# A fused attention and MLP block on one core: the head-pair loop written out, es transposed behind qe, and each score and weight block taken out of PSUM by one masked product of 384 columns

## The reference, cut to what matters

```python
xn = layernorm(x)
q, k, v, g = (xn @ W.T per head for W in (Wq, Wk, Wv, Wg)); q, k = rope(q), rope(k)
s   = clip(xn @ Ws1.T @ Ws2.T + bs2, -32, 32)        # per head: T x 64
es  = exp(s); enz = 1 / cumsum(es)                   # exp(-cumlogsumexp(s))
A   = tril(q @ k.T * DK ** -0.5)                     # 256 x 256, lower triangle
ok  = enz * (A @ es)
qv  = softmax(ok)
W2  = tril((qv * enz) @ es.T)                        # 256 x 256, lower triangle
o   = W2 @ v
out_a = (rmsnorm(o) * g_norm * silu(g)) @ Wo.T
out_m = (gelu(xn @ Wgate.T) * (xn @ Wup.T)) @ Wdown.T   # 4-bit weights, decoded in the kernel
out = x + out_a + out_m
```

## Time and profile before

| | before |
|---|---|
| Median of 3 runs | 1187.22 us |
| The profiled execution, its own time | 1186.13 us |
| Its span, first to last instruction | 1184.4 us |
| Mean granted TensorE clock, share of full | 0.986 |
| TensorE busy (matmul) | 1114.7 us, 94% |
| VectorE busy | 943.1 us, 80% |
| ScalarE busy | 642.1 us, 54% |
| GpSimd busy | 419.6 us, 35% |

### The profile page before, as it was taken

The page is one execution under the profiler, slowest core; times in us unless marked ns, Lnnn a source line. Parts: engine busy times, 40 slices in busy tenths (PEclk is TensorE's granted clock), DMA queues, the critical chain, the costliest instruction groups (busy, mean ns, idle before and its releaser), DMA issues.

```text
span 1184.4 us, 20879 instructions
## 1 busy us (share of the span) xinstructions
PE 1114.7 (94%) x6872; PEld 941.6 (79%) x6872; DVE 943.1 (80%) x1808; ACT 642.1 (54%) x1748; POOL 419.6 (35%) x306
## 2 busy tenths in 40 slices
PE   6789999999999998999989999899998999999995
PEld 5568888888788887888878888788887888788884
DVE  6888887888868887888877888778886888877763
ACT  5355564655645565555655556464563565655451
POOL 5233242433513335232443324343251433523231
PEclk9899999999999999999999999999999999999998
DMA  4001000100001000010000100001000100000001
GB/s 157 1 1 74 1 1 1 52 22 1 1 2 73 1 1 2 1 73 1 1 3 1 74 1 1 3 16 59 1 1 2 73 1 1 1 2 19 1 19 36
DMA packets 9117, 23.19 MB, mean 20 GB/s; under 512 B 816, under 2 KB 5808, under 8 KB 7984
## 3 DMA queue, kind: packets, MB, share of 16 engines
q1 hardware_dynamic: 9008, 21.76, 5.0%
HBM read 19.66 MB, written 2.10 MB: 18 GB/s over the span
## 4 chain that ended last, share of the span: by engine, by line
PE 71%; issue 8%; DVE 6%; ACT 6%; POOL 3%; POOLq 0%; DVEq 0%; ACTq 0%
PE bank L203 17%; PE bank L205 16%; PE bank L204 16%; PE bank L292 5%; ACT xs L568 3%; PE bank L305 3%; PE bank L349 2%; DVE xs L860 2%; POOL qkT L1087 2%; PE bank L294 2%; DVE Wt L740 2%; ACT xs L567 2%; PE bank L282 1%; PE bank L338 1%; PE bank L341 1%
## 5 line engine op out<-in xcount | busy, mean ns | idle before, releaser
L1096 POOL TENSOR_TENSOR inter_lo<-ffb,inter_hi 128x512 fp32r<-128x512 f32 x64 | 83.3, 1323 | 433.2 <-ACT inter_hi L617 433.2
L1087 POOL TENSOR_TENSOR qkT<-ra,xs 128x512 f32<-128x512 f32 x128 | 163.5, 1277 | 95.1 <-DVE xs L860 67.6
L586 ACT ACTIVATE sm<-bank,mx 128x64 f32<-128x64 f32 x256 | 76.3, 325 | 168.5 <-DVE mx L816 168.5
L857 DVE TENSOR_TENSOR ra<-bank,rope 128x512 f32<-128x512 f32 x128 | 88.0, 687 | 55.1 <-ACT xs L568 54.9
L805 DVE RECIPROCAL enzT<-enzT 128x256 f32<-128x256 f32 x64 | 111.6, 1744 | 0.0
L860 DVE TENSOR_TENSOR xs<-xs,rope 128x512 f32<-128x512 f32 x128 | 109.0, 852 | 0.0
L203 PE MATMUL bank<-xh,wqk_hi 128*128 128x512 f32 x256 | 107.4, 420 | 0.0
L203 PE MATMUL bank<-xh,wgu_hi 128*128 128x512 f32 x256 | 106.9, 418 | 0.0
L591 ACT ACTIVATE At<-bank 128x128 f32<-128x128 f32 x128 | 35.4, 276 | 132.0 <-DVE At L740 132.0
L205 PE MATMUL bank<-xh,wgu_lo 128*128 128x512 f32 x256 | 101.6, 397 | 0.0
L203 PE MATMUL bank<-wvg_hi,xh 128*128 128x512 f32 x256 | 101.4, 396 | 0.0
(11 more groups left out here) (137 smaller groups left out, 3211.5 us busy)
## 6 DMA issues: line engine op xcount, KB each, us to landing
raw<-in_w_qkvg SPq DMA_DIRECT2D x8, 1024.0 KB, 4.9
scaled<-in_w_scaled SPq DMA_DIRECT2D x8, 640.0 KB, 7.7
packed<-in_w_packed SPq DMA_DIRECT2D x8, 384.0 KB, 5.4
acc<-in_x SPq DMA_DIRECT2D x4, 512.0 KB, 8.6
out<-acc SPq DMA_DIRECT2D x4, 512.0 KB, 3.0
ws_raw<-in_w_slot SPq DMA_DIRECT2D x8, 48.0 KB, 1.8
rope<-in_rope_tab SPq DMA_DIRECT2D x1, 256.0 KB, 7.0
osq<-in_w_slot SPq DMA_DIRECT2D x1, 128.0 KB, 3.3
```

The source lines that it names most:

```text
L857: dve.tensor_tensor(two(ra[i % 2][:, :]), two(pj[i][:, :]), cos, ALU.mult).then_inc(cos_done, 1)
L1087: pool.tensor_tensor(qkT[:, i, :], ra[i % 2][:, :], xs[i % 2][:, :], ALU.add).then_inc(roped, 1)
L1096: pool.tensor_tensor(inter[1][e][:, :], ffb[e][:, :], inter[0][e][:, :].bitcast(F32), ALU.subtract).then_inc(inter_lo, 1)
```

## The change

The loop is gone: `each_stage` calls `stage` for all eight hp as written-out code, on each engine. `diagonal` becomes `masked`, one VectorE product over all 384 columns with masks whose middle block holds the scale alone, and `off_diagonal` is removed from ScalarE. The semaphores A_out and W_out count the VectorE products and take the place of A_off and W_off. The numbering of the banks is gone: batch b (or head h, for the weights) always uses sc[b] (sc[h]).

The transposes of es move from between `values` 0 and `values` 1 to behind the wait for qe, ahead of `slot_weights` 0, and they go to rg[1], the bank that slot_query has just read. ScalarE's `copy_J` moves ahead to just behind `swap_halves` 1. `slot_weights` 1 moves ahead of `project_qk` 3. On VectorE the last two weight products move ahead of `rope_cos` 2.

```diff
         def each_stage(eng, stage):
-            for bp in range(BP):
-                stage(0, bp, bp == 0, False)
-            with eng.Fori(1, HP - 1) as hp:
+            for hp in range(HP):
                 for bp in range(BP):
-                    stage(hp, bp, False, False)
-            for bp in range(BP):
-                stage(HP - 1, bp, False, bp == BP - 1)
+                    stage(hp, bp, hp == bp == 0, hp == HP - 1 and bp == BP - 1)
...
# TensorE, start of the stage
-                    elif first or i == 1:
-                        pe.wait_ge(J_ready, st + 1)
                     else:
-                        pe.wait_ge(W_off, 4 * st)
+                        pe.wait_ge(W_out, 4 * st - 1 + i)
                     scores(st, bp, i, hp)
...
                 for i in (2, 3):
-                    pe.wait_ge(A_off, 4 * st + i - 1)
+                    pe.wait_ge(A_out, 4 * st + i - 1)
                     scores(st, bp, i, hp)
...
# TensorE, end of the stage
                 pe.wait_ge(qe_ready, st + 1)
-                pe.wait_ge(A_off, 4 * st + 4)
                 if not last:
+                    pe.wait_ge(es_ready, st + 2)
+                    slot_transpose(rg[1], esT[nbp % 2])
                     pe.wait_ge(clip_done, st + 2)
                 slot_weights(st, bp, 0)
                 if not last:
                     project_qk(st + 1, nbp, nhp, 2)
                 if first:
                     transpose_x(3)
+                pe.wait_ge(W_out, 4 * st + 2)
+                slot_weights(st, bp, 1)
                 if not last:
                     project_qk(st + 1, nbp, nhp, 3)
-                pe.wait_ge(W_off, 4 * st + 2)
-                slot_weights(st, bp, 1)
                 pe.wait_ge(v_ready, 4 * st + 4)
...
                 values(st, bp, 0)
-                if not last:
-                    pe.wait_ge(es_ready, st + 2)
-                    pe.wait_ge(W_off, 4 * st + 3)
-                    slot_transpose(sc_bank(bp, "E", 0), esT[nbp % 2])
                 if first:
                     pe.wait_ge(h1_done, 8)
                     pe.wait_ge(h1_lo, 4)
+                elif not last:
+                    pe.wait_ge(J_ready, st + 2)
                 values(st, bp, 1)
...
# ScalarE: the eight off_diagonal copies are dropped, and
                     swap_halves(st + 1, 0)
                     swap_halves(st + 1, 1)
-                off_diagonal(*w_args, 0, 1.0)
-                off_diagonal(*w_args, 1, 1.0)
+                    copy_J(st + 1, rg[1][:, :])
...
# VectorE
-            def diagonal(full, done, dst, bp, kind, st, i, mask, used):
+            def masked(full, done, dst, st, i, mask, used):
                 dve.wait_ge(full, 4 * st + i + 1)
                 wait(dve, *used)
-                src = sc_bank(bp, kind, i)[:, 0:3 * P].rearrange("p (n t) -> p n t", n=3)
-                dve.tensor_tensor(dst[i][:, 0:3:2, :], src[:, 0:3:2, :], mask[:, :, :], ALU.mult).then_inc(done, 1)
+                dve.tensor_tensor(dst[i][:, :, :], sc[i % 2][:, 0:3 * P].rearrange("p (n t) -> p n t", n=3),
+                                  mask[:, :, :], ALU.mult).then_inc(done, 1)
...
-                diagonal(*w_args, 0, mask_w, (o_full, 2 * st))
-                diagonal(*w_args, 1, mask_w, (o_full, 2 * st))
+                masked(*w_args, 0, mask_w, (o_full, 2 * st))
+                masked(*w_args, 1, mask_w, (o_full, 2 * st))
                 if not last:
                     rope_cos(st + 1, 1)
                     rope_sin(st + 1, 1)
                 if first:
                     x_lo(3)
+                masked(*w_args, 2, mask_w, (o_full, 2 * st))
+                masked(*w_args, 3, mask_w, (o_full, 2 * st))
                 if not last:
                     rope_cos(st + 1, 2)
                     rope_sin(st + 1, 2)
-                diagonal(*w_args, 2, mask_w, (o_full, 2 * st))
-                diagonal(*w_args, 3, mask_w, (o_full, 2 * st))
-                if not last:
                     rope_cos(st + 1, 3)
                     rope_sin(st + 1, 3)
```

More of the change, by code:

```diff
@@ L223, in _ @@
                     sp.dma_start(scaled[:, :], w_scaled[0]).then_inc(scaled_in, 16)
-            with sp.Fori(0, HP - 1) as hp:
+            for hp in range(HP - 1):
                 sp.wait_ge(w_lo, 4 * hp + 4)
@@ L276, in slot_scores @@
                     pe.wait_ge(ws2_lo, 4 * hp + 4)
-                pe.matmul(sc_bank((bp - 1) % BP, "S")[:, :] if n is not None else sc[1][:, :],
+                pe.matmul(sc[0][:, :] if n is not None else sc[1][:, :],
                           ws2[:, :], h1[:, bp, :], start=True, stop=True).then_inc(S_full, 1)
@@ L321, in slot_weights @@
                 t0 = b * T
-                pair = [(sc_bank(bp, "W", 2 * b + h), slice(h * M, (h + 1) * M)) for h in range(2)]
+                pair = [(sc[h], slice(h * M, (h + 1) * M)) for h in range(2)]
                 for dst, g in pair:
@@ L427, in stage @@
                 for i in (0, 1):
-                    if first and i == 1:
-                        pe.wait_ge(clip_done, 1)
-                    elif first or i == 1:
-                        pe.wait_ge(J_ready, st + 1)
+                    if first:
+                        pe.wait_ge(clip_done if i == 1 else J_ready, 1)
                     else:
-                        pe.wait_ge(W_off, 4 * st)
+                        pe.wait_ge(W_out, 4 * st - 1 + i)
                     scores(st, bp, i, hp)
@@ L587, in softmax_exp @@
                 ins.then_inc(p_ready, 1)
-            def off_diagonal(diag, done, dst, bp, kind, st, i, scale):
-                act.wait_ge(diag, 4 * st + i + 1)
-                act.activation(dst[i][:, 1, :], sc_bank(bp, kind, i)[:, P:2 * P], ACT.Copy,
-                               scale=scale).then_inc(done, 1)
             def square_o(st, b):
@@ L662, in stage @@
                 npar = (bp + 1) % 2
-                a_args = (A_diag, A_off, At, bp, "A", st)
-                w_args = (W_diag, W_off, Wt, bp, "W", st)
-                more = not (isinstance(hp, int) and hp == HP - 1)
-                off_diagonal(*a_args, 0, SCALE)
-                off_diagonal(*a_args, 1, SCALE)
+                more = hp < HP - 1
                 gate_square(st, 0)
@@ L708, in stage @@
                     split_slot(hp + 1)
+                if not last:
+                    swap_halves(st + 1, 2)
                 if first:
@@ L718, in stage @@
                 square_o(st, 0)
-                if not last:
-                    copy_J(st + 1, sc_bank(bp, "E", 0)[:, :])
                 square_o(st, 1)
@@ L946, in stage @@
                 par, npar, pbp = bp % 2, (bp + 1) % 2, (bp - 1) % BP
-                more = not (isinstance(hp, int) and hp == HP - 1)
-                a_args = (A_full, A_diag, At, bp, "A", st)
-                w_args = (W_full, W_diag, Wt, bp, "W", st)
+                more = hp < HP - 1
+                a_args = (A_full, A_out, At, st)
+                w_args = (W_full, W_out, Wt, st)
                 if bp == 3 and more:
                     slot_lo(hp + 1)
-                diagonal(*a_args, 0, mask_a, (ok_full, st))
+                masked(*a_args, 0, mask_a, (ok_full, st))
                 if not first:
                     sum_squares(st - 1, 1)
-                diagonal(*a_args, 1, mask_a, (ok_full, st))
+                masked(*a_args, 1, mask_a, (ok_full, st))
                 if first:
@@ L965, in stage @@
                     gate_o(npar, 0)
-                diagonal(*a_args, 2, mask_a, (ok_full, st))
+                masked(*a_args, 2, mask_a, (ok_full, st))
                 if not first:
@@ L969, in stage @@
                 gate_gelu(st, 0)
-                diagonal(*a_args, 3, mask_a, (ok_full, st))
+                masked(*a_args, 3, mask_a, (ok_full, st))
                 hidden(st, 0)
@@ L1110, in _ @@
             for m in (mask_a, mask_w):
-                ins = pool.affine_select(out=m[:, :, :], in_=m[:, :, :], compare_op=ALU.is_ge, fill=0.0, base=0,
+                ins = pool.affine_select(out=m[:, 0:3:2, :], in_=m[:, 0:3:2, :], compare_op=ALU.is_ge, fill=0.0, base=0,
                                          pattern=[[0, 2], [1, P]], channel_multiplier=-1)
```

52 lines of the change are left out of this document (21 added, 31 removed).

## The result

The changed kernel takes 1168.47 us (median of 4 runs, 1168.23 to 1168.72) against 1187.70 us (1184.56 to 1188.98) for the kernel before: ratio 0.984, interval 0.982 to 0.986. Faster, but by 19 us where 33 were forecast, and 1168.5 lies just outside the range of 1143 to 1167. The profiled execution took 1168.44 us, with a span of 1166.7 us and a mean granted clock of 0.986.

What follows compares the result with a forecast made beforehand. The prediction saw TensorE as 94% busy, its waits filling the rest, with VectorE at 80%. From 1186.1 us, -16.8 - 25.5 + 2.8 + 7.7 = -31.8 gave 1154 us, range 1143 to 1167.

Steps and rivals of the forecast that it cites:

- The removed waits: TensorE's es transposes waiting for ScalarE's off-diagonal weight copy, 25.5 us, and the written-out loop's 16.8 us would go.
- The loop: Head-pair loop written out: five issue gaps, 10.5 us, and slow clock behind four boundaries, 6.3 us, would go; together -16.8 us.
- Extra changes of matmul kind: Parted projections 2 and 3 on TensorE add one three-pass/float32 change in each of 31 stages: +2.8 us, up to 6.
- The new wait at the gated transposes: VectorE's lag makes TensorE's gated transposes wait in three stages of four, 1.0 us per head pair: +7.7 us, bounds 0 to 23.
- Prologue and tail: Code ahead of and behind the steady stages: -1 to +1 us, priced among the edits at nothing.
- The sum: From the profiled execution's 1186.1 us: -16.8 - 25.5 + 2.8 + 7.7 = -31.8 us, giving 1154.3 us.
- What stood at nothing: ScalarE's 8 dropped copies per stage, the fixed banks, and the second slot_weights' wait for weight products were priced at 0.
- W_out's thin cover: Second slot_weights: weight products 0 and 1 end 0.35 to 0.4 us ahead of project_qk 2's end; taken as 0.
- A: Rival: no new wait at the gated transposes, VectorE's lag staying under the room; 1147 us, or 1144; chance 0.15.
- B: Rival: wait returns at second slot_weights, or gated transposes wait 0.5 us more in three of four stages; 1163-1166 us; chance 0.13.
- C: Rival: written-out code pays for instruction fetches in straight running, so the loop's 16.8 us stay away; 1171 us; chance 0.04.
- D: Rival: VectorE bounds each stage's front, a 384-column product costing more than its columns say; about 1190 us at 0.7; chance 0.03.

Runs made afterwards that it cites:

- the short split: Changed kernel with GpSimd's split of the MLP's gate and up weights, for later head pairs, made on 64 of 512 columns: 1158.89 us, 0.9757.
- norm first: Changed kernel with VectorE's second sum of squares and norm_arg moved ahead of score products 0 and 1: 1155.40 us, 0.9739.
- the added wait: Kernel with the order chosen by stage (1149.65 us), with GpSimd's first wvg_lo split waiting for VectorE's first normalise: 1149.39 us, 0.967.
- the old order: Changed kernel with project_qk 3 again ahead of slot_weights 1, weight products 2 and 3 behind sin 2: 1156.31 us; with blocks split between VectorE and ScalarE again, 1178.98 us.

## Why the prediction was wrong, by its own steps

**The removed waits.** Right. With 33.73 us as the undisturbed stage, the 27 pitches from 90.00 to 1042.15 held 952.15 - 27 x 33.73 = 41.4 us of loss. My terms for that stretch were 16.8 and 27/31 of 25.5, 39.0 us. All of it went.

**The loop, -16.8 us.** As a term of a sum it was right, as a price of its own it was not. It is worth 5 us alone, 3.8 us in the changed kernel, and 17.7 us where nothing else waits. I had given the whole slow clock to the jumps, while in the profiled execution of the written-out code alone it fell at 7 of 7 boundaries. The clock fell behind TensorE gaps of 2.0 to 2.5 us, whoever made them, but not behind all: in the kernel before it stayed whole behind five of the seven es gaps at boundaries, of 2.10 to 2.12 us.

**Extra changes of matmul kind, +2.8 us.** Too high. A plain stage of before is 34.08 less its es wait of 0.36 us, 33.72 us, and 33.73 after. The parted projections cost nothing that shows.

**The new wait at the gated transposes, +7.7 us: this is the step that failed.** The place was right, and for the stage that was worked through the size was near. There the gated transposes were to come 8.61 us behind the first scores, 0.44 us late, and came 8.78 us behind them (395.28 to 404.06), 0.61 us late. But for each head pair the sum is 0.61 + 0.68 + 1.23 + 0.07 = 2.6 us and not 1.0; over the 27 pitches 18.4 us (929.11 - 27 x 33.73) and not 6.7. Of the missing 1.6 us the boundary holds the most, 0.9 us. There I took 0.3 us by a guess, though I had written that VectorE would still be behind the held sin 2, and that the hold "no longer stands in front of" the weight products. The latter is true, but the held sin 2 then stands in front of the norm chain, and the short split shows what this costs, 9.6 us. The earlier trace rows held the answer: a hold of 1.7 us on an engine that has 0.7 us of room at the next narrow place cannot be free. The next 0.4 us are from bp 2 to bp 3, where 0.2 to 0.3 us were forecast and 0.68 measured; that they too hang on the norm chain standing behind A0 and A1 is shown by norm first, which takes all of them away. The last 0.2 us are in the stage that was worked through and, 0.07 us, in the pitch behind the boundary, where nothing was forecast.

**Prologue and tail, -1 to +1 us.** Wrong: 4.7 us were lost ahead of the first gated transposes, and 0.7 us behind st 28, where one pitch at a low clock hides what the edits won. In the three kernels with a loop (the one before, and two of the experiments) the first normalise takes 1.77 or 1.78 us. In all ten without a loop and without the added wait it takes 3.80 to 3.93: the first weights are split earlier there (ScalarE starts on them at 7.9 to 8.3 us, at 9.45 to 9.9 with the loop), and GpSimd's part falls into the midst of normalise. Writing the loop out costs 3.2 us here alone (93.18 against 90.00) and 2.2 us in the changed kernel (94.69 against 92.52). The other 2.5 us come with the rest of the change (92.52 against 90.00). With the loops kept TensorE waits in the first stage 0.9 us for a weight product, 1.2 us for xl (the low part of x) and 1.8 us ahead of values 1, where the kernel before waits only 0.3 us ahead of values; its wait for og, 2.6 us, is down to 0.6. No run takes these apart.

**The sum**, for the profiled execution. In the 27 pitches I had -39.0 for the removed waits, +2.4 for the kinds and +6.7 for the new wait, -29.9 us; measured were -41.4 and +18.4, -23.0 us. Outside them I had the other 1.9 us of gain; measured were 4.7 + 0.7 us of loss. The first is 6.9 us short and the second 7.3, which with rounding makes -17.7 of -31.8. The new wait alone is 11.7 us over its term; 2.4 us of the removed waits and 2.4 us of the kinds, both better than forecast, hide part of it.

**What stood at nothing.** W_out's thin cover held (2.0 us in two waits, first and last stage). ScalarE's copies were not shown to be nothing: in the old order they and VectorE's shorter products together decide whether sin 2 starts ahead of the split or behind, 22.7 us.

**The rivals.** A, the change without the new wait, is what norm first made of the stages inside a head pair; with the boundary and the first stage still losing it took 1155.4 us and not 1147. B came nearest: its place was named rightly, gated transposes, three stages of four, and the 12 us that it gave them are what the wait cost over its term (11.7 us); its time, 1163 to 1166, lacks the loss in the first stage. C fell as stated: no issue waits inside stages but one of 1.8 us in the first, which is there with the loops kept too, and the page shows 55 instruction fetches for 66. D fell, 0.551 us for a product.

## What to carry to other kernels

When a stall is moved behind an operation, follow it to the next narrow place and give it its whole length there; a hold between VectorE and GpSimd is decided by who starts first: sin 2 0.18 us ahead of the split or 0.55 us behind it stood for 22.7 us over this kernel. Price a loop, a wait or a slow clock as removed last, not alone: overlapping causes each look large in the table and small when taken away one at a time. Take the pitch of a stage in which nothing waits and subtract it from every pitch: it gives the whole loss, also the 0.22 us behind each wait that the shown idle leaves out. Take all starts from one view: in the chain a start behind a wait and one without are set differently.

## What the runs showed of the hardware

- rope_sin (two inputs in SBUF) took 2.34 to 2.54 us when it started 0.37 to 0.56 us behind GpSimd's split of the MLP weights, and 0.77 us when it started 0.18 us ahead. It ended 0.55 us behind the split's end each time that it was held. The split took 2.36 us when first and 2.81 us when second. The four tensor_scalar of normalise were held too, 3.8 to 3.9 us for 1.78.
- Groups of eight 128-column transposes took 1.03 us, and 1.09 us behind a wait; a wait cost some 0.22 us more than its shown idle.
- A jump back of the loop cost TensorE 2.4 us where nothing else waited. The granted clock was down behind three of five such gaps (2.26 to 2.42 us; not behind 2.12 and 2.15), behind seven of seven es gaps of 2.0 to 2.3 us in one kernel, two of seven of 2.0 to 2.1 us in another, and six of seven gaps of 2.0 to 2.3 us ahead of values 1 in a third. In the 4 us behind the gaps of 0.45, 0.48 and 1.02 us, and of 1.56 to 1.80 us where the loop was kept in the changed kernel, it stayed at 1.00.
- Straight code brought the first weights in some 1.5 us earlier, and that made the first stage longer: with the split made to wait for normalise, 1.8 us of it were gone.
